# Values folded per head in 16 parts instead of 15 chunks, and the first piece of the down weight clipped on VectorE, scaled and placed by ScalarE

## The chip, the cores and the metric

The kernel runs on one core of one Trainium2 chip. The metric is the device time of one execution in microseconds (us), and the median of several executions is compared. The engines are TensorE (PE, with its weight loads shown as PEld), VectorE (DVE), ScalarE (ACT), GpSimd (POOL) and SyncE (SP), which here only issues transfers (DMA).

## The reference, cut to what matters

The block is a gated cross-attention followed by a feed-forward layer with ternary weights, over 4 batches of 2048 tokens of width 512. The context of a batch has 77 keys of width 384, and there are 8 heads of width 64.

```python
x = x + tanh(g_xattn[0]) * xattn(layernorm(x), ctx_768, Wq, Wk, Wv, Wo, bo)
x = x + tanh(g_ffn[0]) * ffn(layernorm(x), w_gate, w_up, w_down)
# xattn: softmax(q k^T / 8) v per head, then @ Wo + bo
# ffn:   h = relu(bitlinear(x, w_gate))**2 * bitlinear(x, w_up); bitlinear(h, w_down)
def act_quant(x):
    scale = 127.0 / clip(max(abs(x), axis=-1), EPS, None)
    return clip(round(x * scale), -128.0, 127.0) / scale
def weight_quant(w):
    scale = 1.0 / clip(mean(abs(w)), EPS, None)
    return clip(round(w * scale), -1.0, 1.0) / scale
```

Each weight matrix of the feed-forward layer has one unit, the mean of its magnitudes, so no element can be rounded before all of the matrix has been read.

## The kernel before, in words

The 8192 tokens are 64 tiles of 128 tokens. Two things are folded ahead of the tiles. For every batch the keys are multiplied into Wq (`fold_keys`, a matrix "a" of 512 by 616, since 8 heads by 77 keys are 616 columns), and the values into Wo (`fold_values`, a matrix of 616 by 512). Attention of a tile is then two products: tokens with "a" (`make_scores`), probabilities with the folded values (`attend`). Both run on fp32 operands split into a high and a low part.

The folded matrices of batch 0 go straight to where they are used (`first_keys`, `first_values`, and the `_low` functions on VectorE). Those of batches 1 to 3 are evacuated from PSUM by ScalarE (`take_keys`, `take_values`) into small slots of SBUF and stored to DRAM by SP (`store_keys`, `store_values`), to be loaded again when their batch begins (`load_keys`, `load_values`). `fold_values(b, c)` works on a chunk of up to 128 of the 616 rows: GpSimd first writes a matrix `v_pairs` with zeros in which each head's values have rows of their own (`place_values`), and a chunk takes one or two matmuls of 128 rows, depending on how many head pairs it touches. There are three slots for evacuated chunks, in the later-used tile `x1`.

The three feed-forward weights come in 4 pieces of 1 MB each, and every piece passes through four stages: it is loaded, its magnitudes are summed (`measure`, on ScalarE or VectorE), once the unit is known it is scaled with a rounding constant added (`scale`, on ScalarE or VectorE), and two VectorE instructions remove the constant, clip to plus and minus one and write bf16 (`ternary`). The unit of matrix m (0 gate, 1 up, 2 down) comes from `sum_rows(m)`, a matmul `total(m)` and `find_unit(m)`. A piece of the down weight is loaded into the place that a piece of the up weight has left, which ties `load_down` to `ternary(1, ...)`. `relu_half` of the first tile writes its result into the same memory as piece 0 of the down weight, and so waits for `ternary(2, 0)`.

Nothing is scheduled by a planner. Each engine has a list written out by hand for the time ahead of the tiles, and then steps, one per tile, numbered from `s.opens(0)` for tile 0. In step t PE does the first half of gate and up for tile t (`gate_up(s, 0)`), attention of tile t+1, scores of tile t+3, the second half of gate and up, and the down product of tile t-1. Steps 0 and 1 have lists of their own on VectorE (`first_step`, `second_step`), step 1 also on ScalarE. Semaphores hold the order between engines; on an engine the list order is strict, so an instruction that waits holds back all behind it. SP's list is strict as well, and it contains the transposing transfers (`turn_probs` for the probabilities, `turn_input`, `turn_hidden`). On ScalarE the probabilities pass through `part_probs` (planes), the transposing transfer, `join_probs` (probs_t) and `probs_high` (pt_high).

## Time and profile before

| | us |
|---|---|
| median of 3 runs | 1191.43 (1191.32 to 1191.89) |
| profiled execution, its own time | 1190.42 |
| span of the profiled execution, first to last instruction | 1188.6 |
| PE busy | 1174.0 (99%) |
| DVE busy | 1033.9 (87%) |
| ACT busy | 869.2 (73%) |
| first gate matmul of tile 0, 1, 2, 3 | 85.13, 99.97, 118.10, 136.20 |

The profiled execution is 1.0 us under the median, and its time is 1.8 us more than its span. Times in the trace count from the start of the span. What lies ahead of 85.13 us is the preparation; from there on PE works on tiles.

### The profile page before, as it was taken

To read this page: it belongs to the slowest core of one execution; us is meant where nothing else is said; L and a number is where in the kernel's file an instruction comes from. 1 tells how busy PE (TensorE), PEld (TensorE's weight loads), DVE (VectorE), ACT (ScalarE), POOL (GpSimd) and SP (SyncE) were. 2 spreads that over 40 slices of the span, in tenths; PEclk is the share of its full clock that TensorE was granted. 3 is DMA by queue.
4 is the path that set the end of the run, shared out by engine and by line. 5 is a ranking of instruction groups with operands and counts; after the bars stand their busy time and mean duration, and the time that the engine had idled before them with its cause. 6 is when DMAs were issued, how large, how long until landed. Compare 5 with 4: busy or idle time off the path is not lost.

```text
span 1188.6 us, 18855 instructions
## 1 busy us (share of the span) xinstructions
PE 1174.0 (99%) x5867; PEld 744.8 (63%) x5867; DVE 1033.9 (87%) x2124; ACT 869.2 (73%) x929; POOL 307.2 (26%) x313
## 2 busy tenths in 40 slices
PE   9989999999999999999999999999999999999998
PEld 7656656665665666566566656666665666666554
DVE  4989898888988888888998888889899888988887
ACT  5877777776887677677877767776787777677764
POOL 3222222222442222222442222222244222222200
DMA  9793554444444464444444464443444444444333
GB/s 356 262 297 77 156 147 100 98 111 97 97 112 102 126 158 114 96 108 97 101 100 101 115 179 108 98 110 93 101 113 101 100 97 110 97 101 108 84 65 76
DMA packets 286485, 144.71 MB, mean 122 GB/s; under 512 B 254586, under 2 KB 255226, under 8 KB 283889
## 3 DMA queue, kind: packets, MB, share of 16 engines
q1 hardware_dynamic: 286445, 144.32, 47.7%
q8 instruction: 11, 0.18, 0.1%
q14 instruction: 25, 0.20, 0.1%
q10 hardware_dynamic: 4, 0.00, 0.0%
HBM read 57.86 MB, written 24.35 MB: 69 GB/s over the span
## 4 chain that ended last, share of the span: by engine, by line
PE 86%; DVE 7%; ACT 3%; issue 2%; DMA 1%; POOL 0%; DVEq 0%; ACTq 0%; POOLq 0%
PE gu_ps L1084 34%; PE o_ps L1048 17%; PE y_ps L1098 17%; PE s_ps L66 17%; DVE half_max L1330 1%; DVE staged L1324 1%; DMA staged<-in_wd_t 1%; PE gu_ps L1148 1%; PE gu_ps L1208 1%; DMA a_scr<-a_spare 0%; DVE w_up L1484 0%; DVE staged L1456 0%; ACT staged L778 0%; DVE w_down L1484 0%; ACT x_marked L854 0%
## 5 line engine op out<-in xcount | busy, mean ns | idle before, releaser
L1084 PE MATMUL gu_ps<-w_up,xq_t 128*128 128x512 bf16 x1024 | 241.9, 379 | 1.9 <-DVE staged L1324 1.9
L1084 PE MATMUL gu_ps<-w_gate,xq_t 128*128 128x512 bf16 x1016 | 240.9, 380 | 1.3 <-DMA xq_t<-xq 1.2
L1098 PE MATMUL y_ps<-w_down,hq_t 128*128 128x512 bf16 x1008 | 227.8, 379 | 0.0
L1048 PE MATMUL o_ps<-v_sb,pt_high 128*128 128x512 f32 (+1 forms) x640 | 212.8, 413 | 0.9 <-DVE pt_low L1313 0.9
L1324 DVE TENSOR_TENSOR staged<-staged,gu_ps 128x1024 f32<-128x1024 f32 x128 | 155.6, 1216 | 53.5 <-ACT staged L784 53.5
L66 PE MATMUL s_ps<-a_sb,xf_high 128*128 128x308 f32 x1024 | 187.4, 305 | 0.0
L1084 PEld LDWEIGHTS gu_ps<-w_up,xq_t 128*128 128x128 bf16 x1024 | 100.0, 98 | 123.6 <-DVE staged L1324 3.8
L645 POOL TENSOR_TENSOR rstd<-var_eps,neg_half 128x1 f32<-128x1 f32 x128 | 96.4, 753 | 307.1 <-DVE var_eps L1289 274.6
L824 ACT ACTIVATE staged<-staged,h_scale 128x1024 f32<-128x1024 f32 x126 | 137.9, 1142 | 48.9 <-DVE h_scale L1344 48.9
L1098 PEld LDWEIGHTS y_ps<-w_down,hq_t 128*128 128x128 bf16 x1008 | 98.8, 98 | 118.8
L778 ACT ACTIVATE staged<-gu_ps 128x1024 f32<-128x1024 f32 x127 | 128.9, 1015 | 52.4 <-PE gu_ps L1084 52.0
L1084 PEld LDWEIGHTS gu_ps<-w_gate,xq_t 128*128 128x128 bf16 x1016 | 94.3, 98 | 113.5 <-DMA xq_t<-xq 2.8
L66 PEld LDWEIGHTS s_ps<-a_sb,xf_high 128*128 128x128 f32 x1024 | 159.7, 188 | 6.0 <-issue 0.5
L1330 DVE TENSOR_REDUCE half_max<-staged 128x1 f32<-128x1024 f32 x128 | 155.4, 1214 | 2.3
L791 ACT ACTIVATE planes<-probs 128x1280 int16<-128x1280 int16 x63 | 80.0, 1269 | 104.7 <-POOL probs L650 104.7
L626 POOL TENSOR_TENSOR xf_low<-xf_sb,xf_high 128x512 fp32r<-128x512 f32 x64 | 82.7, 1292 | 275.9 <-ACT xf_high L694 275.9
L650 POOL TENSOR_TENSOR probs<-probs,prob_inv 128x616 f32<-128x616 f32 x64 | 78.3, 1223 | 257.1 <-DVE prob_inv L1308 257.1
L1048 PEld LDWEIGHTS o_ps<-v_sb,pt_high 128*128 128x128 f32 (+1 forms) x640 | 120.6, 189 | 34.5 <-issue 1.4
L784 ACT ACTIVATE staged<-staged 128x1024 f32<-128x1024 f32 x128 | 134.8, 1053 | 2.2
L1048 PE MATMUL o_ps<-v_sb,pt_low 128*128 128x512 f32 (+1 forms) x320 | 127.1, 397 | 0.0
L66 PE MATMUL s_ps<-a_sb,xf_low 128*128 128x308 f32 x512 | 113.9, 303 | 0.0
L800 ACT ACTIVATE probs_t<-planes_t 128x1280 int16<-128x1280 int16 x63 | 104.1, 1652 | 0.4 <-DMA planes_t<-planes 0.4
(146 smaller groups left out, 1438.8 us busy)
## 6 DMA issues: line engine op xcount, KB each, us to landing
xf_sb<-in_x_feat SPq DMA_DIRECT2D x64, 256.0 KB, 2.6
x_sb<-in_x_tok SPq DMA_DIRECT2D x64, 256.0 KB, 2.9
y<-staged SPq DMA_DIRECT2D x63, 256.0 KB, 2.0
staged<-in_wg_t SPq DMA_DIRECT2D x4, 1024.0 KB, 9.5
staged<-in_wd_t SPq DMA_DIRECT2D x4, 1024.0 KB, 7.6
folded<-a_scr SPq DMA_DIRECT2D x3, 1232.0 KB, 5.6
v_scr<-x SPq DMA_DIRECT2D x12, 256.0 KB
folded<-v_scr SPq DMA_DIRECT2D x3, 1024.0 KB, 5.1
```

The costliest lines, as they stand in the source:

```text
L66: last = nc.tensor.matmul(s_ps[:, n, 0:HALF_KEYS], x_part[:, c, :], a_sb[:, a, c, n * HALF_KEYS:(n + 1) * HALF_KEYS], start=(c == 0 and x_ ...
L626: nc.gpsimd.tensor_tensor(xf_low[:, s.par(d), :, :], xf_sb[:, :, :], xf_high[:, s.par(d), :, :].bitcast(F32), ALU.subtract).then_inc(xf_lo ...
L645: nc.gpsimd.tensor_tensor(rstd[:, :], var_eps[:, :], neg_half[:, :], ALU.pow).then_inc(done, 1)
L778: nc.scalar.activation(relu, last_gate_ps if at_end else gate_ps, ACT.Relu).then_inc(relu_done[n], 1)
L784: nc.scalar.activation(relu_sq, relu, ACT.Square).then_inc(square_done[n], 1)
L800: nc.scalar.activation(probs_t_halves, planes_t_by_half, ACT.Copy).then_inc(probs_joined, 1)
L824: nc.scalar.activation(h_marked[:, cols], hidden[:, cols], ACT.Copy, bias=ROUND, scale=h_scale[:, 0:1]).then_inc(h_marked_done[n], 1)
L1048: last = nc.tensor.matmul(o_ps[:, :], pt[0:rows, P * c:P * (c + 1)], v_sb[0:rows, v, c, :], start=(c == 0 and pt is pt_high and v == 0), s ...
L1084: last = nc.tensor.matmul(target[:, q, :], xq_t[:, s.par(0), c, :], w[:, c, cols], start=(c == 0), stop=(c == DC - 1))
L1098: last = nc.tensor.matmul(y_ps[:, :], hq_t[:, c, :], w_down[:, c, :], start=(c == 0), stop=(c == FC - 1))
L1324: nc.vector.tensor_tensor(hidden[:, cols], relu_sq, last_up_ps if at_end else up_ps, ALU.mult).then_inc(hidden_done[n], 1)
L1330: nc.vector.tensor_reduce(half_max[:, n:n + 1], hidden[:, cols], axis=AX, op=ALU.max, apply_absolute_value=True).then_inc(half_max_done, 1)
```

## The change

It has five parts.

The values of batches 1 to 3 are no longer folded through `v_pairs`. A part k (of 16) is half the keys of one head, over the three batches together: 231 keys in 116 and 115 rows. Its matmul contracts the head's 64 rows of `v_t` directly, so there are 16 matmuls with 64 rows of contraction where there were 24 with 128, and GpSimd's `place_values` is done once instead of four times. A part spans two batches, so it is stored with two transfers of 77 and 39, or 38 and 77, rows: 32 stores instead of 15. The evacuated parts have seven places: three in `x1`, and four more in `bo_sb`, `probs_t` and `k_pairs` (in the first use order 0, 1, 2, 3, 4).

The first piece of the down weight is loaded into `v_pairs`, which is free once batch 0 is folded, and no longer waits for an up piece. VectorE clips it to plus and minus the unit in one instruction (`clip_first_down`); ScalarE scales it (`mark_first_down`) and later takes the rounding constant off, writing bf16 (`place_first_down`). `relu_half` of tile 0 now waits for `ternary(1, 2)`, the up piece that last used its memory, and the first `down` waits for PLACED.

SP queues all eight gate and up pieces at once, ahead of the first wait. Which engine measures or scales which piece changes: VectorE measures 6 and scales 5 (before 4 and 7), ScalarE measures 6 and scales 6 plus the two new passes (before 8 and 5). The lists ahead of the tiles are reordered on all engines.

ScalarE gets its own `first_step`, and VectorE's `first_step` is reordered. `second_step` and all later steps are as before. In DRAM the folded values now lie row by row.

```diff
-V_OUT_RING = 3
+V_PLACE = [0, 1, 2, 3, 4, 0, 1, 2, 3, 4, 0, 1, 2, 3, 5, 6]
...
+def head_part(k):
+    h, s = divmod(k, 2)
+    return h, KEYS + FIRST_ROWS * s, FIRST_ROWS - s
...
         def raw(m, p):
+            if m == 2 and p == 0:
+                return v_pairs[:, :, :].rearrange("p q n -> p (q n)")[:, 0:PIECE]
...
                 def load_down(p):
-                    sp.wait_ge(weight_stage[1][UP_SLOT.index(p)], DONE)
+                    if p == 0:
+                        sp.wait_ge(vo_done, KC)
+                    else:
+                        sp.wait_ge(weight_stage[1][UP_SLOT.index(p)], DONE)
...
+                def store_later_values(k):
+                    at = KEYS * head_part(k)[0]
+                    sp.wait_ge(vo_taken, k + 1)
+                    for b, j, n, r in part_runs(k):
+                        sp.dma_start(v_scr[b, at + j:at + j + n, :].rearrange("p (q n) -> p q n", q=HP),
+                                     v_slots[V_PLACE[k]][r:r + n, :, :]).then_inc(v_stored[V_STORE[k]], 16)
...
+                def fold_later_values(k):
+                    h, first, rows = head_part(k)
+                    if k < V_RING:
+                        pe.wait_ge(v_split_done, KC + k - V_RING + 1)
+                    else:
+                        pe.wait_ge(vo_taken, k - V_RING + 1)
+                    own = slice(HEAD * (h % 2), HEAD * (h % 2 + 1))
+                    nc.tensor.matmul(value_slots[(KC + k) % V_RING][0:rows, :], v_t[own, h // 2, first:first + rows], wo_sb[own, h // 2, :],
+                                     start=True, stop=True, tile_position=(HEAD * (h % 2), 0)).then_inc(vo_done, 1)
...
+                def clip_first_down():
+                    nc.vector.tensor_scalar(neg_unit[:, :], unit[:, 2:3], -1.0, None, ALU.mult).then_inc(unit_done, 1)
+                    dve.wait_ge(unit_done, 4)
+                    dve.wait_ge(weight_stage[2][0], MEASURED)
+                    nc.vector.tensor_scalar(raw(2, 0), raw(2, 0), unit[:, 2:3], neg_unit[:, 0:1],
+                                            ALU.min, ALU.max).then_inc(weight_stage[2][0], 1)
...
                     if s.opens(0) and n == 0:
-                        wait(act, weight_stage[2][0], DONE)
+                        wait(act, weight_stage[1][UP_SLOT.index(0)], DONE)
...
+                def first_step(s):
+                    relu_half(s, 0)
+                    square_half(s, 0)
+                    mark_first_down()
+                    scale(2, 2)
+                    part_probs(s, 2)
+                    scale(2, 3)
+                    mark_input(s, 1)
+                    join_probs(s, 2)
+                    probs_high(s, 2)
+                    high_part(s, 4)
+                    relu_half(s, 1)
+                    square_half(s, 1)
+                    place_first_down()
+                    exponentials(s, 3)
```

On ScalarE, this is the end of the preparation and step 0 of the kernel before (L812 `probs_high`, L791 `part_probs`, L778 and L784 `relu_half` and `square_half`, L730 `scale`, L800 `join_probs`, L854 `mark_input`, L694 `high_part`).

```order
L812 ACTIVATE pt_high<-probs_t 128x640
L791 ACTIVATE planes<-probs 128x1280
L778 ACTIVATE staged<-gu_ps 128x1024
L784 ACTIVATE staged<-staged 128x1024
L730 ACTIVATE staged<-staged,inv_unit 128x2048 x2
L800 ACTIVATE probs_t<-planes_t 128x2x640
L812 ACTIVATE pt_high<-probs_t 128x640
L854 ACTIVATE x_marked<-centred,x_scale 128x512
L694 ACTIVATE xf_high<-xf_sb 128x512
L778 ACTIVATE staged<-gu_ps 128x1024
L784 ACTIVATE staged<-staged 128x1024
```

The same place of the changed kernel (L858 `probs_high`, L813 `exponentials`, L823 and L829 `relu_half` and `square_half`, L764 `mark_first_down`, L757 `scale`, L836 `part_probs`, L900 `mark_input`, L846 `join_probs`, L721 `high_part`):

```order
L813 ACTIVATE probs<-probs,rstd 128x616
L823 ACTIVATE staged<-gu_ps 128x1024
L829 ACTIVATE staged<-staged 128x1024
L764 ACTIVATE v_pairs<-v_pairs,inv_unit 128x2048
L757 ACTIVATE staged<-staged,inv_unit 128x2048
L836 ACTIVATE planes<-probs 128x1280
L757 ACTIVATE staged<-staged,inv_unit 128x2048
L900 ACTIVATE x_marked<-centred,x_scale 128x512
L846 ACTIVATE probs_t<-planes_t 128x2x640
L858 ACTIVATE pt_high<-probs_t 128x640
L721 ACTIVATE xf_high<-xf_sb 128x512
L823 ACTIVATE staged<-gu_ps 128x1024
```

The planes of tile 2 were made ahead of the first relu; now they come after it, its square and two passes over a weight piece.

On VectorE, this is step 0 of the kernel before from the second half of its list on (L1423 `unmark_input`, L1302 `shift_scores`, L1330 `top_half`, L1484 and L1487 `ternary`, L1324 `hidden_half`, L1313 `probs_low`, L1337 to L1344 `hidden_scales`).

```order
L1423 TENSOR_SCALAR xq<-x_marked 128x512
L1302 TENSOR_TENSOR probs<-s_ps,score_max 128x616
L1330 TENSOR_REDUCE half_max<-staged 128x1
L1484 TENSOR_SCALAR w_down<-staged 128x2048
L1487 TENSOR_SCALAR w_down<-w_down 128x2048
L1324 TENSOR_TENSOR staged<-staged,gu_ps 128x1024
L1313 TENSOR_TENSOR pt_low<-probs_t,pt_high 128x640
L1484 TENSOR_SCALAR w_down<-staged 128x2048
L1487 TENSOR_SCALAR w_down<-w_down 128x2048
L1330 TENSOR_REDUCE half_max<-staged 128x1
L1337 TENSOR_REDUCE h_max<-half_max 128x1
```

The same place of the changed kernel (L1369 `top_scores`, L1399 `hidden_half`, L1377 `shift_scores`, L1388 `probs_low`, L1405 `top_half`, L1567 and L1570 `ternary`, L1412 `hidden_scales`):

```order
L1369 TENSOR_REDUCE score_max<-s_ps 128x8
L1399 TENSOR_TENSOR staged<-staged,gu_ps 128x1024
L1377 TENSOR_TENSOR probs<-s_ps,score_max 128x616
L1388 TENSOR_TENSOR pt_low<-probs_t,pt_high 128x640
L1405 TENSOR_REDUCE half_max<-staged 128x1
L1567 TENSOR_SCALAR w_down<-staged 128x2048
L1570 TENSOR_SCALAR w_down<-w_down 128x2048
L1567 TENSOR_SCALAR w_down<-staged 128x2048
L1570 TENSOR_SCALAR w_down<-w_down 128x2048
L1405 TENSOR_REDUCE half_max<-staged 128x1
L1412 TENSOR_REDUCE h_max<-half_max 128x1
```

Three pieces of work (the shift of the scores, the first half's maximum and one ternary piece) stood ahead of the second `hidden_half`; now all of them stand behind it.

## Rows read from the trace of the kernel before

**Rows 1.** The page's first line and its busy times by engine.
```profile
span 1188.6 us, 18855 instructions
PE 1174.0 (99%) x5867; PEld 744.8 (63%) x5867; DVE 1033.9 (87%) x2124; ACT 869.2 (73%) x929; POOL 307.2 (26%) x313
```

**Rows 2.** Windows: stretch, its length, busy time by engine, granted clock, DMA share, GB/s.
```profile
0.00:85.13 85.13, 78.35 (x354) 56.19 (x354) 62.60 (x97) 58.37 (x81) 27.04 (x41) 1.00 0.88 306
...
154.59:1188.00 1033.41, 1028.92 (x5182) 646.94 (x5180) 907.56 (x1902) 758.41 (x795) 264.64 (x257) 1.00 0.44 107
```

**Rows 3.** Timeline of PE: start, busy, instruction, in brackets idle before and releaser.
```profile
85.13 1.90 PE L1084 MATMUL gu_ps<-w_gate,xq_t 128*128 128x512 bf16 x8
...
118.10 1.90 PE L1084 MATMUL gu_ps<-w_gate,xq_t 128*128 128x512 bf16 x8
```

**Rows 4.** Timeline of ACT around step 0.
```profile
76.76 1.91 ACT L720 ACTIVATE hq_t<-staged 128x2048 bf16<-128x2048 f32 x1 [3.19 <-DMA staged<-in_wd_t]
...
88.07 1.03 ACT L778 ACTIVATE staged<-gu_ps 128x1024 f32<-128x1024 f32 x1 [0.34 <-DVE w_down L1487]
...
90.10 3.89 ACT L730 ACTIVATE staged<-staged,inv_unit 128x2048 f32<-128x2048 f32 x2
93.89 1.65 ACT L800 ACTIVATE probs_t<-planes_t 128x1280 int16<-128x1280 int16 x1
95.58 0.74 ACT L812 ACTIVATE pt_high<-probs_t 128x640 fp32r<-128x640 f32 x1
...
96.89 0.61 ACT L694 ACTIVATE xf_high<-xf_sb 128x512 fp32r<-128x512 f32 x1
```

**Rows 5.** Timeline of DVE, preparation.
```profile
23.73 1.51 DVE L1491 TENSOR_TENSOR a_sb<-gu_ps,a_sb 128x616 fp32r<-128x616 f32 x2 [2.06 <-ACT a_sb L736]
...
49.56 0.15 DVE L1467 TENSOR_SCALAR unit<-y_ps 128x1 f32<-128x1 f32 x1
...
69.29 2.23 DVE L1446 TENSOR_REDUCE part_sums<-staged 128x4 f32<-128x2048 f32 x1
71.44 0.68 DVE L1357 TENSOR_TENSOR x<-x_sb,o_ps 128x512 f32<-128x512 f32 x1
...
74.87 0.79 DVE L1294 TENSOR_REDUCE score_max<-s_ps 128x8 f32<-128x616 f32 x1
...
76.41 0.20 DVE L1384 TENSOR_SCALAR x_top_n<-x_top,rstd 128x1 f32<-128x1 f32 x1
```

**Rows 6.** Timeline of DVE, step 0.
```profile
97.36 0.79 DVE L1302 TENSOR_TENSOR probs<-s_ps,score_max 128x616 f32<-128x616 f32 x1
98.07 1.21 DVE L1330 TENSOR_REDUCE half_max<-staged 128x1 f32<-128x1024 f32 x1
99.20 1.22 DVE L1484 TENSOR_SCALAR w_down<-staged 128x2048 bf16<-128x2048 f32 x1
...
101.06 1.21 DVE L1324 TENSOR_TENSOR staged<-staged,gu_ps 128x1024 f32<-128x1024 f32 x1
102.19 0.82 DVE L1313 TENSOR_TENSOR pt_low<-probs_t,pt_high 128x640 fp32r<-128x640 f32 x1
...
106.03 0.15 DVE L1337 TENSOR_REDUCE h_max<-half_max 128x1 f32<-128x2 f32 x1
...
106.67 0.21 DVE L1344 TENSOR_SCALAR h_scale<-h_inv,hidden_scale 128x1 f32<-128x1 f32 x1
```

**Rows 7.** Groups of instructions by form, 40 to 90 us: busy, mean ns.
```profile
L1208 PE MATMUL gu_ps<-folded,v_pairs 128*128 128x512 f32 x42 | 19.5, 601 | 3.1 <-ACT x L762 3.1
...
L762 ACT ACTIVATE x<-gu_ps,gate_tanh 128x512 f32<-128x512 f32 x12 | 8.0, 677 | 0.3 <-PE gu_ps L1208 0.2
...
L791 ACT ACTIVATE planes<-probs 128x1280 int16<-128x1280 int16 x2 | 2.5, 1266 | 0.0
...
L650 POOL TENSOR_TENSOR probs<-probs,prob_inv 128x616 f32<-128x616 f32 x2 | 2.4, 1217 | 9.0 <-DVE prob_inv L1308 9.0
```

**Rows 8.** The tile planes_t, 0 to 200 us: its transposing transfers.
```profile
DMA to landing us min/median/max: 3.4/3.4/6.5
```

More of the change, by code:

```diff
@@ L912, in step @@
                         mark_hidden(s, -1)
-                    if s.has(0):
+                    if s.has(0) and not s.opens(0):
                         relu_half(s, 0)
@@ L955, in _ @@
                 gate_bias()
-                high_part(start, 1)
                 first_keys(2)
@@ L1645, in _ @@
-                dve.wait_ge(tanh_done, 1)
-                first_values_low(0)
-                measure(0, 3)
-                first_values_low(1)
-                sum_probs(start, 0)
-                sum_rows(0)
-                first_values_low(2)
+                measure(1, 0)
+                sum_rows(1)
+                ternary(0, 0, w_gate)
+                scale(0, 1)
+                find_unit(1)
+                find_hidden_unit()
+                probs_low(start, 0)
+                ternary(0, 1, w_gate)
@@ L1652, in _ @@
+                ternary(0, 2, w_gate)
+                scale(1, 2)
+                scale(1, 0)
+                ternary(1, 3, w_up)
+                ternary(1, 0, w_up)
+                ternary(1, 1, w_up)
+                add_attention(start, 0)
+                input_scale(start, 0)
+                top_scores(start, 1)
+                shift_scores(start, 1)
+                unmark_input(start, 0)
+                sum_probs(start, 1)
+                ternary(1, 2, w_up)
                 dve.wait_ge(rstd1_done, 2)
```

429 lines of the change are left out of this document (219 added, 210 removed).

## The prediction

> **What bounds the kernel now.** I read the page first: PE is busy 1174.0 of 1188.6 us [rows 1]. The windows say where the rest is. From 154.59 us on PE is busy 1028.92 of 1033.41 us, so whatever a change wins or loses before that is passed on almost whole to the end; in the preparation it is busy 78.35 of 85.13 [rows 2]. Everything the change touches in time lies before about 118 us, since the second step and all later ones have the lists they had. So I follow three marks: R, the start of the first relu (88.07 us, [rows 4]); H, the end of the first h_scale, 106.67 + 0.21 = 106.88 us [rows 6]; and the first gate matmul of tile 2, 118.10 us [rows 3]. VectorE passes H on through the unchanged second step (unmark, second `hidden_half`, attention and input scale of tile 2, its transposing transfer), and the gate of tile 2 follows H by 118.10 - 106.88 = 11.2 us.
>
> What stands before R: the last down piece is measured only when it has landed, after ScalarE idled 3.19 us [rows 4]; then come the down unit, two scales and `ternary(2, 0)` on VectorE, and relu waited 0.34 us for that ternary [rows 4]. The preparation is thus bounded by VectorE and the chain of down pieces, not by PE.
>
> **The change part by part.**
>
> Fewer folds. A fold matmul leaves two records: 42 of them took 19.5 us, so one matmul takes 19.5 / 21 = 0.9 us [rows 7]. 24 matmuls become 16. If 64 rows of contraction cost as much as 128, PE saves 8 x 0.9 = 7.2 us; if half, 14. PE idled 3.1 us in front of these matmuls for ScalarE [rows 7], and ScalarE now evacuates 16 parts instead of 15 chunks, 0.7 us more [rows 7]. Since PE does not bound R, I count neither saving. The Trainium skill, TensorEngine Tiling (Array Packing), section Key Properties, says that a change of tiling mode drains TensorE, which speaks against 16 matmuls of 64 rows among matmuls of 128. No row here shows such a drain. It would come out of the 7.2 us that I do not count.
>
> When the up unit is found (t1, 49.56 us, [rows 5]). Ahead of it VectorE now has one more measure (2.2 us, [rows 5]), one `input_stats` less (about 1.1: a pass of 0.7 as in the row at 71.44 and two small ones) and no `probs_low` (0.8, [rows 6]): 0.3 us more work. Against it stand VectorE's waits, such as the 2.06 us at 23.73 [rows 5]. With eight pieces queued without a wait, none of the waits for a landing should last. I take t1 = 48.8, bounds 45 (most of some 4 us of waits gone) and 50.
>
> From t1 to R. VectorE then has, up to the end of the sums of tile 1: small unit instructions 0.8, `probs_low` 0.8, five ternary pieces of 101.06 - 99.20 = 1.9, which is 9.3 [rows 6], two scales of the length of the row at 99.20, 2.4 [rows 6], attention and input scale 74.87 - 71.44 = 3.4, top and shift 76.41 - 74.87 = 1.5 [rows 5], `unmark_input` with its wait for ScalarE 0.8, the sums 1.0: 20.0 us. Then the chain goes over to ScalarE's strict list: normalise on GpSimd 1.2, planes 1.3 [rows 7], `measure(2, 1)` 2.1, `high_part` 0.6 [rows 4], the last five evacuations (two of keys, three of values) at 0.7 = 3.5 [rows 7], a microsecond of waiting for PE's last folds, probs_t 1.7 and pt_high 0.7 [rows 4], exponential 0.8: 12.9 us. So R = 48.8 + 20.0 + 12.9 = 81.7 at the earliest with t1 as taken. VectorE must in the same time have done the fourth up ternary, statistics, two measures and the shift of tile 2 behind the sums: 1.9 + 1.1 + 4.4 + 1.6 = 9.0 us, under the 12.9 minus the final exponential, so it fits. None of these sums holds a stall, and before the same kind of chain had several between 49.56 and 88.07. I add 2.8 us (two waits of a microsecond or so, and rows that run long beside other engines) and take R = 84.5, which is 3.6 us earlier than before. Bounds: 79 with t1 = 45 and half the stalls, 88 if a landing stays on the path as now.
>
> What leaves the path: `ternary(2, 0)` and the down scales no longer stand before R. Were the new down path slow, it would show only at the first down product, where before the hidden transposes came last; the clip costs one pass of the length 1.2 [rows 6], or 2.2 if it runs at the rate of a measure [rows 5], on VectorE between R's shift and step 0, where its cover is ScalarE's 3.2 us of probs_t, pt_high and exponential. `place_first_down`, 1.9 to 2.0 (3.89 / 2, [rows 4]), stands behind the second square, while VectorE does the work below.
>
> From R to H, step 0. Before: 106.88 - 88.07 = 18.8 us. Now ScalarE does relu and square (90.10 - 88.07 = 2.0), two passes of 3.89 / 2 each (93.89 - 90.10 = 3.8), and only then the planes, 1.3 [rows 4, 7]: R + 7.1. The transposing transfer takes 3.4 to 6.5 us to landing [rows 8]; I take 3.4, since the stores and the two token loads ahead of it are some 8 us old by then: R + 10.6 with its start. `scale(2, 3)` and `mark_input` (2.7 us) hide under it. probs_t 1.7, pt_high 0.7, `high_part` 0.6 [rows 4]: the second relu starts at R + 13.6 although PE has its input since about R + 10. Square ends at R + 15.7. VectorE has nothing else ahead in its list and waits for that square from about R + 12 on. Behind it: `hidden_half` 1.1 (102.19 - 101.06), shift 0.7, `probs_low` 0.7, maximum 1.1 (99.20 - 98.07), two ternary pieces 3.7, maximum 1.2, `hidden_scales` 0.9 (106.88 - 106.03) [rows 6]: 9.5 us. H = R + 25.2. That is 6.4 us more than before. The cause is visible in the order: before, 3.7 us of shift, maximum and ternary filled the time in which ScalarE was not ready, and the planes had been made before the first relu.
>
> Sum: H = 84.5 + 25.2 = 109.7, against 106.88: 2.8 us later, and the gate of tile 2 with it, at 120.9. The profiled execution of 1190.42 us would become 1193.2; on the median, 1.0 higher, 1194.2. Batch loads of the folded values (now 2 KB rows) lie under ten tiles of work and count nothing; if one came late it would show at the first tile of a batch.
>
> SP issues 32 stores for 15, 17 x about 0.45 us = 8 us more of issue, spread over 45 us; the first transposing transfer behind them (tile 2's) waits for planes anyway, so it costs nothing unless SP falls more than 5 us behind.
>
> **The rivals.**
>
> Balance: R at 81.7, as the bare sum says, or a stall less in step 0; then H is 106.9 and the time is 1191.4. It is the forecast without the 2.8 us of stalls.
>
> Faster: the waits of VectorE before t1 vanish. Working without a break it would reach t1 near 45 and, with the bare sum, R = 78; H = 103.2, 3.7 us early: 1187.7. It decides from R = 79.3 on (2.4 us early at H). For it: all eight pieces are queued early, and DMA moved only 306 GB/s over the preparation at a share of 0.88 [rows 2]. Against: the 2.06 us wait is one for ScalarE's key evacuation and a fold, which the change leaves in place [rows 5].
>
> Much slower: the stores hold the loads back. 38 rows are 19 x 2, and 77 are 7 x 11, so such pieces may not use all sixteen DMA engines. If 38 rows lie on two engines, each gets 39 KB; at 306 / 0.88 / 16 = 22 GB/s per engine [rows 2] that is 1.8 us for each of eight such stores, and every load behind waits for those two. Two such delays on the path, at the third down piece and at R, give 3.6 us more: R = 88.1, 1197.8. It takes over from the forecast at R = 86.7, where H is 5 us late. The Trainium skill, DMA: Bandwidth & Descriptors, section Why a DMA increments its semaphore by 16 and not by 1, says just this of the split: the largest number up to 16 that divides the outer size, which is 2 for 38 rows, 11 for 77 and 13 for 39. The stores before had 128 and 104 rows, and no row of this trace shows a piece on few engines.
>
> The change does not do what it says: should folds of 64 rows take 0.9 us and evacuations stay as many, the fold part changes nothing on the path; this is already in the forecast.
>
> **How the numbers follow.** A measurement of this kernel tells 0.2% (2.4 us) from no change. Forecast 0.60, with its own range 1191.9 to 1196.5 (H + 0.5 to + 5), of which 0.36 lie above 1193.8 and 0.24 below; balance 0.12; faster 0.13; much slower 0.15. So slower 0.36 + 0.15 = 0.51, same 0.24 + 0.12 = 0.36, faster 0.13. The range goes from 1189.0, inside the faster case, to 1198.5, past the much slower one.
>
> **What would show it.** Right: relu of tile 0 near 84.5 us, a wait of ScalarE's probs_t for planes_t and of VectorE's second `hidden_half` for the square (3 to 5 us) in step 0, an h_scale near 109.7, the gate of tile 2 near 120.9, and the same spacing from there on. Wrong: relu before 80 us or after 87; a transposing transfer of 5 us or more in step 0 (1.6 us more); stalls of folds on `v_stored`; late landings of down pieces. If the gate of tile 2 is late but the end is not, PE made it up later, which would overturn the first step of the argument.

## The result, and the profile after

The changed kernel takes 1194.31 us (median of 18 executions, 1192.11 to 1196.87) where the kernel before took 1191.34 (18, 1188.74 to 1192.93): a ratio of 1.0029, 95% interval 1.0022 to 1.0035, or 3.0 us more. The profiled execution of it took 1195.31 us, which is 1.0 above its median, where that of before lay 0.9 below its own; so the two traces are 4.9 us apart, 1.9 more than the medians. Part of that surplus goes with the clock, as the rows below show.

The page of the changed kernel, with the clock that was granted:

```profile
span 1193.5 us, 18761 instructions
...
PE 1169.3 (98%) x5786; PEld 741.2 (62%) x5851; DVE 1036.3 (87%) x2124; ACT 871.7 (73%) x929; POOL 299.5 (25%) x301
...
PEclk9989999999999999999999999999999999999999
```

PE bounds the kernel as in [rows 1]. TensorE's timeline (start, us, instruction, idle time before it and who ended it) has the marks that answer to [rows 3]:

```profile
73.95 1.11 PE L1283 MATMUL gu_ps<-folded,v_t 64*115 64x512 f32 x2
77.06 1.53 PE L1252 MATMUL gu_ps<-k_pairs,folded 128*128 128x154 f32 x8 [2.00 <-ACT folded L793]
78.52 3.76 PE L1283 MATMUL gu_ps<-folded,v_t 64*116 64x512 f32 x4
...
83.04 3.19 PE L1149 MATMUL gu_ps<-w_gate,xq_t 128*128 128x512 bf16 x7 [0.24 <-issue]
86.02 3.00 PE L1149 MATMUL gu_ps<-w_up,xq_t 128*128 128x512 bf16 x8
...
122.98 1.90 PE L1149 MATMUL gu_ps<-w_gate,xq_t 128*128 128x512 bf16 x8 [1.03 <-DMA xq_t<-xq]
```

The gate of tile 2 starts at 122.98 us, 4.9 later than the 118.10 of before, and this is just what the execution is longer by: nothing is made up afterwards. ScalarE, for [rows 4], and then VectorE, for [rows 6]:

```profile
86.27 1.03 ACT L823 ACTIVATE staged<-gu_ps 128x1024 f32<-128x1024 f32 x1 [0.27 <-PE gu_ps L1149]
...
92.08 1.25 ACT L836 ACTIVATE planes<-probs 128x1280 int16<-128x1280 int16 x1
96.10 0.72 ACT L900 ACTIVATE x_marked<-centred,x_scale 128x512 f32<-128x512 f32 x1 [0.86 <-DVE x_scale L1454]
96.91 1.65 ACT L846 ACTIVATE probs_t<-planes_t 128x1280 int16<-128x1280 int16 x1
...
99.75 1.01 ACT L823 ACTIVATE staged<-gu_ps 128x1024 f32<-128x1024 f32 x1
```

```profile
92.54 0.69 DVE L1432 TENSOR_TENSOR x<-x_sb,o_ps 128x512 f32<-128x512 f32 x1 [1.52 <-PE o_ps L1113]
...
101.88 1.22 DVE L1399 TENSOR_TENSOR staged<-staged,gu_ps 128x1024 f32<-128x1024 f32 x1 [2.54 <-ACT staged L829]
...
111.19 0.21 DVE L1419 TENSOR_SCALAR h_scale<-h_inv,hidden_scale 128x1 f32<-128x1 f32 x1
```

R, the first relu, is at 86.27 us (88.07 before). The planes of tile 2 are made at R + 5.8, the second relu at R + 13.5, VectorE waits 2.54 us for the square, and H, the end of h_scale, is at 111.19 + 0.21 = 111.40: H - R is 25.1 us where it was 18.8. One sign that was forecast is missing here: ScalarE's probs_t does not wait for its transposing transfer, since x_marked ahead of it had waited 0.86 us for VectorE. In e1, e3, e4 and e5 the wait is there, about 1.05 us.

One thing stands in this trace that the trace of before has not: the clock fell. Windows of two microseconds (sum, busy time of the engines, then granted clock, DMA share, GB/s):

```profile
74.00:76.00 2.00, 1.06 (x3) 0.22 (x2) 1.97 (x3) 2.00 (x4) 0.55 (x1) 1.00 1.18 135
76.00:78.00 2.00, 0.94 (x7) 0.94 (x8) 2.00 (x2) 1.58 (x3) 1.27 (x1) 1.00 1.38 52
78.00:80.00 2.00, 2.00 (x5) 0.99 (x5) 1.83 (x4) 0.68 (x1) 0.00 (x0) 0.50 0.85 161
...
86.00:88.00 2.00, 2.00 (x6) 0.76 (x5) 2.00 (x3) 1.70 (x2) 0.00 (x0) 0.50 0.38 109
88.00:90.00 2.00, 2.00 (x9) 1.38 (x8) 1.93 (x4) 2.00 (x2) 1.63 (x1) 0.94 0.29 81
```

PE idled 2.00 us ahead of the key fold at 77.06, then the granted clock was 0.50 for ten microseconds, the lower of its two levels (1.2 instead of 2.4 GHz): eight up matmuls took 3.00 us, where all later ones take 1.89. Of the 18 executions 8 had a mean clock of 0.999 and took 1192.11 to 1194.17 us, 1193.4 in the mean; the 10 others had 0.995 to 0.997 and took 1194.22 to 1196.87, 1195.4 in the mean. The profiled one (0.996) is of the second kind; the profile of before shows 1.00 throughout.

### The profile page after: what moved, and what is told of

Its sections match the earlier page's. It is cut to its first block, busy times and chain, and to the rows that moved or that the text cites. A ratio compares the mean times of both kernels' runs of the same rounds, so it can differ in the third digit from the quotient of the medians.

```text
span 1193.5 us, 18761 instructions
## 1 busy us (share of the span) xinstructions
PE 1169.3 (98%) x5786; PEld 741.2 (62%) x5851; DVE 1036.3 (87%) x2124; ACT 871.7 (73%) x929; POOL 299.5 (25%) x301
## 4 chain that ended last, share of the span: by engine, by line
PE 84%; DVE 6%; ACT 3%; DMA 3%; issue 2%; SPq 1%; ACTq 0%; DVEq 0%
PE gu_ps L1149 33%; PE o_ps L1113 17%; PE y_ps L1164 17%; PE s_ps L71 16%; DMA staged<-in_wg_t 2%; DVE half_max L1405 1%; DMA v_scr<-bo_sb 1%; DVE staged L1399 1%; ACT staged L823 1%; DVE w_gate L1567 0%; DVE w_up L1567 0%; ACT probs_t L846 0%; ACT staged L829 0%; DVE pt_low L1388 0%; PE gu_ps L1283 0%
## 5 line engine op out<-in xcount | busy, mean ns | idle before, releaser
L1149 PE MATMUL gu_ps<-w_gate,xq_t 128*128 128x512 bf16 x951 | 227.9, 381 | 7.9 <-DMA xq_t<-xq 1.6
L1399 DVE TENSOR_TENSOR staged<-staged,gu_ps 128x1024 f32<-128x1024 f32 x128 | 155.6, 1215 | 54.4 <-ACT staged L829 54.4
L823 ACT ACTIVATE staged<-gu_ps 128x1024 f32<-128x1024 f32 x127 | 129.0, 1016 | 49.6 <-PE gu_ps L1149 49.6
L836 ACT ACTIVATE planes<-probs 128x1280 int16<-128x1280 int16 x63 | 79.9, 1269 | 107.1 <-POOL probs L680 107.1
L1405 DVE TENSOR_REDUCE half_max<-staged 128x1 f32<-128x1024 f32 x128 | 155.3, 1214 | 2.3
L829 ACT ACTIVATE staged<-staged 128x1024 f32<-128x1024 f32 x128 | 134.8, 1053 | 2.2
L846 ACT ACTIVATE probs_t<-planes_t 128x1280 int16<-128x1280 int16 x63 | 104.0, 1651 | 0.3 <-DMA planes_t<-planes 0.2
```

Of the source, the lines that this page charges most:

```text
L823: nc.scalar.activation(relu, last_gate_ps if at_end else gate_ps, ACT.Relu).then_inc(relu_done[n], 1)
L829: nc.scalar.activation(relu_sq, relu, ACT.Square).then_inc(square_done[n], 1)
L846: nc.scalar.activation(probs_t_halves, planes_t_by_half, ACT.Copy).then_inc(probs_joined, 1)
L1149: last = nc.tensor.matmul(target[:, q, :], xq_t[:, s.par(0), c, :], w[:, c, cols], start=(c == 0), stop=(c == DC - 1))
L1399: nc.vector.tensor_tensor(hidden[:, cols], relu_sq, last_up_ps if at_end else up_ps, ALU.mult).then_inc(hidden_done[n], 1)
L1405: nc.vector.tensor_reduce(half_max[:, n:n + 1], hidden[:, cols], axis=AX, op=ALU.max, apply_absolute_value=True).then_inc(half_max_done, 1)
```

## The experiments

Theory: the change wins time before R and gives back more in step 0, by VectorE's new order and ScalarE's late planes. Rivals: the clock; stores on few DMA engines; TensorE's 64-row mode; ScalarE's new passes. Twelve kernels were run, each timed beside the kernel before. Ratios are to before, with the 95% interval; R, H and the start of tile 2's gate are from one profiled execution each.

| kernel | ratio | interval | R | H | H - R | gate of tile 2 |
|---|---|---|---|---|---|---|
| before | 1 | | 88.07 | 106.88 | 18.8 | 118.10 |
| changed | 1.0029 | 1.0022 to 1.0035 | 86.27 | 111.40 | 25.1 | 122.98 |
| e1 order on VectorE | 1.0005 | 0.9996 to 1.0014 | 83.32 | 105.75 | 22.4 | 117.34 |
| e2 planes first | 1.0061 | 1.0047 to 1.0075 | 91.82 | 114.58 | 22.8 | 126.16 |
| e3 PE busy | 1.0023 | 1.0012 to 1.0034 | 84.12 | 109.21 | 25.1 | 120.79 |
| e4 full rows | 1.0028 | 1.0017 to 1.0039 | 85.05 | 110.14 | 25.1 | 121.71 |
| e5 rows 109, 122 | 1.0020 | 1.0011 to 1.0029 | 84.01 | 109.10 | 25.1 | 120.67 |
| e6 rows 114, 117 | 1.0098 | 1.0083 to 1.0114 | 90.88 | 117.94 | 27.1 | 129.53 |
| e7 e1 and PE busy | 0.9994 | 0.9985 to 1.0003 | 84.71 | 107.14 | 22.4 | 118.73 |
| e8 before, new order | 1.0011 | 1.0002 to 1.0021 | 89.09 | 110.39 | 21.3 | 121.62 |
| e9 e1 and e5 | 1.0008 | 0.9999 to 1.0017 | 84.80 | 107.20 | 22.4 | 118.78 |
| e10 e7 and e5 | 1.0002 | 0.9993 to 1.0011 | 86.82 | 109.25 | 22.4 | 120.83 |
| e11 e9 and planes early | 1.0032 | 1.0019 to 1.0045 | 85.81 | 110.28 | 24.5 | 121.87 |
| e12 first piece on VectorE | 1.0030 | 1.0021 to 1.0040 | 83.29 | 108.84 | 25.6 | 120.07 |

**e1, VectorE's order of step 0.**

```diff
                     top_scores(s, 3)
-                    hidden_half(s, 1)
                     shift_scores(s, 3)
-                    probs_low(s, 2)
                     top_half(s, 0)
                     ternary(2, 2, w_down)
+                    hidden_half(s, 1)
+                    probs_low(s, 2)
                     ternary(2, 3, w_down)
```

> The changed kernel with VectorE's list of the first step in the order of before in one respect: shift, first maximum and the third down ternary stand ahead of the second hidden_half again, and everything else is as changed. Theory A (what VectorE does while ScalarE is not ready is the cost): 3.7 us of work move into the idle time of about 2.5 to 5 us ahead of the second hidden_half, so h_scale comes 3.5 us after R earlier than in the changed kernel, H - R goes from 25.1 to about 21.5, the gate of tile 2 comes near 119.3 us and the time falls from 1194.3 to about 1190.8, a ratio of 0.9995 to before. Theory B (the late planes on ScalarE are the whole cost): the second hidden_half waits for ScalarE as before and what stands behind it is no shorter than what ScalarE and PE need; H - R stays at 24 to 25 and the ratio at 1.002 to 1.003.

The order alone takes the ratio from 1.0029 to 1.0005; theory B's 1.002 is outside the interval, and theory A's 0.9995 just below its lower end. R came at 83.32 in this profile although nothing ahead of it was changed, so H - R is what the edit is judged by. The profiled execution took 1190.33 us, that of before 1190.42. VectorE and GpSimd of this kernel:

```profile
88.37 0.68 DVE L1432 TENSOR_TENSOR x<-x_sb,o_ps 128x512 f32<-128x512 f32 x1
...
97.02 2.27 DVE L1567 TENSOR_SCALAR w_down<-staged 128x2048 bf16<-128x2048 f32 x1
99.32 0.69 DVE L1570 TENSOR_SCALAR w_down<-w_down 128x2048 bf16<-128x2048 bf16 x1
99.93 1.21 DVE L1399 TENSOR_TENSOR staged<-staged,gu_ps 128x1024 f32<-128x1024 f32 x1
...
105.54 0.21 DVE L1419 TENSOR_SCALAR h_scale<-h_inv,hidden_scale 128x1 f32<-128x1 f32 x1
```

```profile
96.94 1.27 POOL L656 TENSOR_TENSOR xf_low<-xf_sb,xf_high 128x512 fp32r<-128x512 f32 x1 [1.88 <-ACT xf_high L721]
98.16 1.89 POOL L675 TENSOR_TENSOR rstd<-var_eps,neg_half 128x1 f32<-128x1 f32 x1
```

The wait for the square is gone and H comes 2.7 us sooner after R, 0.9 short of the 3.6 expected. The rest went into the ternary at 97.02, which took 2.27 instead of 1.22 us while GpSimd worked beside it, and whose neighbour on GpSimd took 1.89 us where the one before it (94.51) took 0.55. The long ternary comes again in e7, e9 and e10, which have this order too (2.26, 2.25 and 2.28); where GpSimd had nothing beside it, the same instruction took 1.22 (at 101.80 here, at 105.59 in the changed kernel). In the kernel before it was GpSimd that came off worse: its power at 98.81 took 1.64 us, and the ternary at 99.20 beside it 1.22. That the two engines hinder each other is read from these coincidences; no run isolates it.

**e2, planes first.**

```diff
+                    part_probs(s, 2)
                     relu_half(s, 0)
                     square_half(s, 0)
-                    mark_first_down()
                     scale(2, 2)
-                    part_probs(s, 2)
                     scale(2, 3)
+                    mark_first_down()
```

> The changed kernel with ScalarE's list of the first step changed back: the planes of tile 2 (part_probs) ahead of the first relu, and mark_first_down behind both scales; VectorE's list as changed. Theory A (planes late cost as much as VectorE's order): H - R falls by 3 us or more and the time by as much, to 1191. Theory B (the sums of tile 2 and GpSimd's normalising are ready only 3 us or so after R in the changed preparation, since VectorE's sum_probs of tile 2 stands behind the clip): the relu is then held up by the planes, R moves from 86.3 to about 90, H - R falls by at most 2, and the time rises by 1 to 3 us, to 1195.5 to 1197 (ratio 1.0035 to 1.005).

Slower, 1.0061, beyond theory B's 1.005, which the interval (from 1.0047) takes in. ScalarE of this kernel:

```profile
90.64 1.27 ACT L836 ACTIVATE planes<-probs 128x1280 int16<-128x1280 int16 x1 [4.51 <-POOL probs L680]
91.82 1.01 ACT L823 ACTIVATE staged<-gu_ps 128x1024 f32<-128x1024 f32 x1
```

ScalarE waits 4.51 us for GpSimd's normalised probabilities with the relu queued behind. H - R falls by 2.4 us, but R comes 5.5 us later than in the changed kernel. In the changed preparation the late place of the planes is what the late sums ask for.

**e3, PE kept busy.**

```diff
+                def keep_busy():
+                    for _ in range(4):
+                        nc.tensor.matmul(y_ps[:, P:3 * P], ones[:, :], wo_sb[:, 0, 0:2 * P], start=True, stop=True)
...
+                keep_busy()
                 fold_keys(3, 3)
```

> The changed kernel with four extra matmuls of 256 float32 columns (product unused, into columns of the bank of y that nobody reads) ahead of the last fold of keys, where PE idled 2.0 us at 75 us. They add work and leave everything else. Theory A (the granted clock fell to 0.50 between 78 and 88 us because PE had idled): the clock stays at 1.00 in every stretch, the two folds and the gate and up matmuls of tile 0 take what they did before (1.9 us for eight records instead of 3.2), R comes 1.5 to 3 us earlier, near 84, the mean granted clock of all executions is 0.999 or more, and the time falls by 1 to 2 us, to 1192.5 to 1193.3 (ratio 1.001 to 1.0018). Theory B (the clock falls by something else, or the drop hides behind ScalarE and VectorE): the same drops are seen, or they go and the time stays within 0.5 us of 1194.3 (ratio 1.0025 to 1.0029).

The ratio, 1.0023, lies between the theories, and its interval takes in both. Between 78 and 88 us the clock stayed at 1.00, and R came at 84.12, 2.2 us earlier, as theory A had it; but the clock fell elsewhere, first behind an idle time of 2.94 us, so the mean clocks are still 0.996 to 0.999:

```profile
98.70 2.69 PE L1149 MATMUL gu_ps<-w_gate,xq_t 128*128 128x512 bf16 x8 [2.94 <-ACT staged L823]
101.18 2.82 PE L1149 MATMUL gu_ps<-w_up,xq_t 128*128 128x512 bf16 x8
...
140.26 3.30 PE L1149 MATMUL gu_ps<-w_gate,xq_t 128*128 128x512 bf16 x8 [2.04 <-DMA xq_t<-xq]
```

**e4, folds over 128 rows.** (Each part then holds the sum of two heads.)

```diff
-                    nc.tensor.matmul(value_slots[(KC + k) % V_RING][0:rows, :], v_t[own, h // 2, first:first + rows], wo_sb[own, h // 2, :],
-                                     start=True, stop=True, tile_position=(HEAD * (h % 2), 0)).then_inc(vo_done, 1)
+                    nc.tensor.matmul(value_slots[(KC + k) % V_RING][0:rows, :], v_t[:, h // 2, first:first + rows], wo_sb[:, h // 2, :],
+                                     start=True, stop=True).then_inc(vo_done, 1)
```

> The changed kernel with its 16 later value folds contracted over all 128 partitions and without a tile position; so each part holds the sum of two heads' values, not the one head's. Columns, rows of the result, order and waits are the same. Theory A (64 rows cost no less than 128, and a change of the tiling mode costs TensorE something at each of the changes): a fold goes from 1.11 us to about 0.95, and the issue waits of 0.77 us of key folds behind it to about 0.24; PE is off the path, so the time changes by less than 1 us (ratio 1.0022 to 1.0030). Theory B (64 rows were cheaper after all, and what I read as 1.11 us is the bare duration): folds take 1.1 us or more as well and nothing changes behind them. If PE's folds do lie on the path to R through ScalarE's waits, the time falls by 1 to 2 us.

1.0028, theory A. The fold matmuls as a group (count of records, then shortest, median and longest duration in ns), and the weight loads of a key fold behind such a fold, with the wait ahead of them; the changed kernel first, then e4:

```profile
L1283 PE MATMUL gu_ps<-folded,v_t x30: 589/682/1199, 40.9 to 81.2; 64*115 64x512 f32 x16, 64*116 64x512 f32 x14
...
65.59 1.08 PEld L1252 LDWEIGHTS gu_ps<-k_pairs,folded 128*128 128x128 f32 x8 [0.77 <-issue]
```

```profile
L1282 PE MATMUL gu_ps<-folded,v_t x30: 591/592/1057, 40.7 to 80.4; 128*115 128x512 f32 x16, 128*116 128x512 f32 x14
...
64.23 0.97 PEld L1252 LDWEIGHTS gu_ps<-k_pairs,folded 128*128 128x128 f32 x7 [0.24 <-issue]
```

A record of 64 rows is no shorter at best (589 against 591 ns) and 90 ns longer at the median, and the key weights behind one wait 0.77 us instead of 0.24. So the new folds save TensorE only their number, and a return to 128 rows costs about half a microsecond (0.77 - 0.24); neither reaches the time. The drain that the Trainium skill, TensorEngine Tiling (Array Packing), section Key Properties, describes agrees with this.

**e5 and e6, the rows of the stores.**

```diff
-FIRST_ROWS = ((BATCH - 1) * KEYS + 1) // 2
+FIRST_ROWS = 109
...
-    return h, KEYS + FIRST_ROWS * s, FIRST_ROWS - s
+    return h, KEYS + FIRST_ROWS * s, ((BATCH - 1) * KEYS - FIRST_ROWS) if s else FIRST_ROWS
```

(114 instead of 109 in e6.)

> The changed kernel with each head's 231 later rows parted into 109 and 122 instead of 116 and 115; so its stores have 77, 32, 45 and 77 rows instead of 77, 39, 38 and 77. Result, number of instructions, order and bytes are the same. Theory A (a store uses as many DMA engines as the largest number up to 16 that divides its rows: 38 rows then sit on two engines, 32 on sixteen, 45 on fifteen, and this held back what lies behind): landings of stores and loads between 36 and 90 us get shorter, ScalarE's waits of 1.0 to 1.5 us for a_scr stores go, R comes 1 to 2 us earlier than the 84.1 to 86.3 us seen in the kernels with the changed preparation, and the time falls by 1 to 2 us, to about 1192.8 (ratio 1.001 to 1.002). Theory B (the split over engines does not reach the path): the ratio stays at 1.0022 to 1.0035.

> The same with 114 and 117 rows: stores of 77, 37, 40 and 77 rows. By theory A the eight stores of 37 rows sit on one DMA engine each, 76 KB, which at about 22 GB/s per engine are 3.4 us each, twice what 38 rows cost on two; 40 rows use ten engines. Then R comes 1 to 3 us later than in the changed kernel (86 to 89 us) and the time is 1195.5 to 1197.5 (ratio 1.0035 to 1.005). By theory B nothing changes against the changed kernel (ratio 1.0022 to 1.0035), and the run before this one is like it too.

With 37 and 40 rows (e6) the time is 11.7 us above before, about twice the upper end of theory A. The mean clocks are lower too, 0.989 to 0.993, so part of it goes with the clock. With 32 and 45 rows (e5) the ratio is 1.0020, the upper end of theory A, but its interval and that of the changed kernel overlap. The landings differ clearly (DMA issues between 36 and 90 us: count, KB each, median us from issue to landing; first the changed kernel, then e5, then e6):

```profile
staged<-in_wd_t SPq DMA_DIRECT2D x3, 1024.0 KB, 9.0
a_scr<-a_spare SPq DMA_DIRECT2D x6, 308.0 KB, 6.2
...
planes_t<-planes SPq DMA_TRANSPOSE x1, 5.6
```

```profile
staged<-in_wd_t SPq DMA_DIRECT2D x3, 1024.0 KB, 6.7
a_scr<-a_spare SPq DMA_DIRECT2D x6, 308.0 KB, 4.1
...
planes_t<-planes SPq DMA_TRANSPOSE x1, 3.7
```

```profile
staged<-in_wd_t SPq DMA_DIRECT2D x3, 1024.0 KB, 10.2
a_scr<-a_spare SPq DMA_DIRECT2D x6, 308.0 KB, 7.4
...
planes_t<-planes SPq DMA_TRANSPOSE x1, 7.3
```

The folded values stored are the same bytes in all three; in the order 32 and 45, 38 and 39, 37 and 40 rows the landings in these rows grow. The kernel before, whose stores had 128 and 104 rows, has 7.6 us for the down pieces and 4.5 for a_spare. In e6 ScalarE idles for its spare slot twice over 2.5 us:

```profile
54.04 0.69 ACT L793 ACTIVATE a_spare<-gu_ps 128x616 f32<-128x616 f32 x1 [2.81 <-DMA a_scr<-a_spare]
...
86.06 0.68 ACT L793 ACTIVATE a_spare<-gu_ps 128x616 f32<-128x616 f32 x1 [4.55 <-DMA a_scr<-a_spare]
```

In the changed kernel the waits for such stores are 1.10, 1.50 and 1.50 us (at 50.44, 53.79 and 79.08); in e5 none is left. This is the ordering that the rule of the Trainium skill on the split over engines, DMA: Bandwidth & Descriptors, section Why a DMA increments its semaphore by 16 and not by 1, gives: 16 and 15 engines, 2 and 13, 1 and 10. The number of engines itself stands in no row.

**e7, e1 with PE's two idle times filled.** To the edits of e1 and e3 comes:

```diff
+                def keep_busy_again(s):
+                    for _ in range(12):
+                        nc.tensor.matmul(y_ps[:, P:], xq_t[:, s.par(0), 0, :], w_gate[:, 0, P:512], start=True, stop=True)
...
+                    if s.opens(0):
+                        keep_busy_again(s)
                     if s.has(0):
                         gate_up(s, 1)
```

> The changed kernel with the order of the first run (shift, maximum and third down ternary ahead of the second hidden_half), with the four extra matmuls before the last fold of keys, and with twelve extra matmuls of 384 columns in the first step, between the scores of tile 3 and the second half of gate and up, where PE idled 2.9 us; their products are not used. Theory A (PE's idle times of 2 us and more are what the granted clock falls after, and such falls cost the mean execution about 1.5 to 2 us, since the executions of the first run at a mean clock of 0.999 took 1190.0 to 1190.8 and those at 0.996 to 0.997 took 1191.8 to 1193.5): all executions show 0.999 or 1.000 and lie at 1189.5 to 1190.8, ratio 0.9985 to 0.9995. Theory B (the falls come from elsewhere, or the extra work costs what it saves): the mean clocks keep scattering from 0.995 to 0.999 and the ratio is 1.000 to 1.0015.

0.9994, the lowest ratio of all and no different from before by a measurement that tells 0.2%; the interval meets that of e1 too. The mean clocks are 0.998 to 1.000 (0.995 to 0.999 in e1), so the clock was low for less of the time; but the profiled execution still shows 0.50 between 70 and 72 us, behind an idle time of 0.82 us at 67.88. Theory A holds in part.

**e8, the new order in the kernel before.**

```diff
                     unmark_input(s, 1)
+                    hidden_half(s, 1)
                     shift_scores(s, 3)
+                    probs_low(s, 2)
                     top_half(s, 0)
                     ternary(2, 2, w_down)
-                    hidden_half(s, 1)
-                    probs_low(s, 2)
```

> The kernel before, with VectorE's first step changed in one respect as the change does it: the second hidden_half ahead of shift, first maximum and third down ternary. Preparation, folds, down pieces and ScalarE's order are those of before. Theory A (this order alone is most of what the change costs in the first step): VectorE then idles some 2 us ahead of the second hidden_half, for ScalarE's second square, which ends near 98 us here; what stands behind it is 3.7 us longer; H comes near 109 instead of 106.88, the gate of tile 2 near 120.3 instead of 118.1, and the time rises by 1.8 to 2.8 us, ratio 1.0015 to 1.0024. Theory B (the order costs only with late planes): H stays within 1 us and the ratio within 0.9995 to 1.0008.

VectorE of this kernel:

```profile
100.86 1.22 DVE L1324 TENSOR_TENSOR staged<-staged,gu_ps 128x1024 f32<-128x1024 f32 x1 [2.40 <-ACT staged L784]
...
110.18 0.21 DVE L1344 TENSOR_SCALAR h_scale<-h_inv,hidden_scale 128x1 f32<-128x1 f32 x1
```

H - R is 21.3 instead of 18.8: 2.5 us, nearly all of it the wait of 2.40. The ratio, 1.0011, is below theory A's 1.0015, with an interval (1.0002 to 1.0021) that takes it in, as it does part of theory B's range; H, 3.5 us later than before, of which 1.0 is R, decides for A. So the order costs the same 2.5 to 2.7 us put into the old kernel or taken out of the new one.

**e9 and e10, the edits together.** e9 is e1 with the rows of e5, e10 is e9 with both `keep_busy` edits of e7.

> The changed kernel with VectorE's order of the first run and the parts of 109 and 122 rows, and no extra matmuls. Theory A (order and store sizes act at different places, R and H - R, and so add): the order alone took 2.2 us off (1.0005), the rows alone some 1 us (1.0020); together 1191.0 or a little less, ratio 0.9990 to 1.0000, with R near 83.5 and H near 105.5. Theory B (the rows only helped by chance of where the clock fell): ratio 1.0002 to 1.0010, as with the order alone.

> The same with the extra matmuls of the seventh run too (four before the last fold of keys, twelve in the first step). If the three act each for itself: order -2.2 us, rows -1, filled idle times -0.7, from 1194.5 to 1190.3 or so, ratio 0.9982 to 0.9992 and the fastest of all. Rival: the extra matmuls delayed ScalarE's last key evacuation by 2.0 us in the profile of the seventh run and so give back what the clock saves; then this run is no faster than the one before it (ratio within 0.0005 of it).

e9 gives 1.0008, no better than e1: theory B, so nothing shows that what e5 seemed to win adds. Windows of e9's profiled execution show that the clock fell in the place where PE had idled, and once more at 98 us:

```profile
66.00:68.00 2.00, 0.60 (x2) 0.00 (x0) 1.86 (x6) 1.23 (x3) 0.14 (x1) 1.00 1.03 434
68.00:70.00 2.00, 1.88 (x2) 0.41 (x2) 1.24 (x3) 1.92 (x4) 0.00 (x0) 0.55 0.96 400
70.00:72.00 2.00, 2.00 (x8) 1.94 (x8) 1.93 (x4) 0.69 (x1) 1.51 (x1) 0.50 0.93 354
```

e10 gives 1.0002, inside the intervals of e7 and e9 both, with R at 86.82, behind ScalarE's key evacuation, which waited 2.28 us for PE and its extra matmuls. Between the theories it decides nothing, except that the sum of all three was too hopeful.

**e11, the planes made possible and made early.** To the edits of e9 (order and rows) comes:

```diff
+                sum_probs(start, 2)
                 clip_first_down()
                 probs_low(start, 1)
                 scale(2, 1)
-                sum_probs(start, 2)
...
                     square_half(s, 0)
+                    part_probs(s, 2)
+                    scale(2, 2)
                     mark_first_down()
-                    scale(2, 2)
-                    part_probs(s, 2)
                     scale(2, 3)
```

> As the first of this set (order and rows), and besides the sums of tile 2 on VectorE ahead of the clip, and on ScalarE the planes of tile 2 right behind the first square, ahead of all three weight passes. Theory A (it was the late planes that made ScalarE's second relu late, and the second run failed only because the sums were late): with the sums 2.5 us earlier the planes start near R + 2 to 3 instead of R + 5.9, the second relu moves from R + 13.5 to about R + 11, and the time falls by another 1 to 2 us below the first of this set. Theory B (the order on VectorE leaves nothing to gain there, and passes that move behind the planes delay both ternary pieces): the second relu comes no earlier than R + 13, H - R grows by 1 to 2 us, and the time rises by as much.

Theory B: the ratio goes from e9's 1.0008 to 1.0032 and H - R from 22.4 to 24.5. The planes go at 88.29 (R + 2.5), and yet the second relu comes at R + 15.1. pt_low stands behind the sums now, so attention on PE waits 2.69 us for it, VectorE reaches x_scale late, and ScalarE waits 2.23 us for that ahead of everything else.

**e12, the first down piece back on VectorE.** `scale(2, 0)` in the place of `clip_first_down()`, `ternary(2, 0, w_down)` ahead of `ternary(2, 1, w_down)`, and:

```diff
                     square_half(s, 0)
-                    mark_first_down()
...
                     square_half(s, 1)
-                    place_first_down()
```

> The changed kernel with the new path of the first down piece undone: VectorE scales it in the place of the clip and makes it ternary (3.1 us in all instead of the 1.35 us of the clip), and ScalarE's two passes for it (2.0 and 1.9 us) are gone; slots, loads and the other orders as changed. Theory A (ScalarE's two passes are on the path of the first step: the planes stand behind one of them): planes, join and second relu come 1 to 2 us earlier, H - R falls from 25.1 to 23.5, the time to about 1192.8 (ratio 1.0010 to 1.0018). Theory B (VectorE needs the 1.8 us that it now has more, so that the move to ScalarE is neutral or a gain): H - R stays within 0.7 us of 25.1 and the ratio is 1.0025 to 1.0040.

1.0030, theory B; H - R is 25.6. The planes do come earlier (R + 4.6), after a wait of 0.60 us for GpSimd's probabilities, but x_marked then waits 2.67 us for VectorE, which reaches it later. Clip and placement by ScalarE are neither the loss nor a gain that these runs can tell.

## Why the prediction was right

It said 1194.2 us, 2.8 more than before, and the median is 1194.31, 3.0 more. Step by step:

**PE bounds, and what is late at tile 2 stays late.** Right: 4.88 us at the gate of tile 2, 4.89 in the execution.

**The up unit, t1.** 48.44 us; 48.8 was taken. VectorE still waited 2.51 us for the landing of an up piece, so queueing all pieces early did not end its waits, and the faster rival failed here:

```profile
27.15 2.29 DVE L1521 TENSOR_REDUCE part_sums<-w_up 128x4 f32<-128x2048 f32 x1 [2.51 <-DMA w_up<-in_wu_t]
```

**From t1 to R.** 37.8 us against 35.7. VectorE's part was mis-sized: 22.1 us for 20.0, since two passes that [rows 6] has at 1.22 took 1.82 and 2.32 (GpSimd worked beside both) and a wait of 0.76 for ScalarE's exponential was missing, of which 0.4 had been allowed beside `unmark_input`. In e5, where the clock was below 1.00 only between 68 and 74 us, R is at 84.01, 35.4 after its up unit: the 2.8 us for stalls covered this. The profiled execution is 2.3 us later; in it the clock was at 0.50 from 78 to 88 us, and ScalarE waited 1.50 us for a store at 79.08. In e3, with the same stores and a clock of 1.00 up to R, R is at 84.12 and that wait is gone too, so the two go together. R near 84.5 is what the executions with no fall before R (e3) or a short one (e1 83.32, e4 85.05, e5, e12 83.29) show. Which part of the change brings R forward from 88.07 is not shown: e4, e5 and e12 each put one part back or alter it, and R stays early; the new lists of the preparation were not taken apart.

**From R to H.** 25.2 was worked out, 25.1 measured, and 25.1 again in e3, e4 and e5 (the items behind the square add up to 9.4 as rounded there, to 9.5 from the rows). The planes were placed at R + 7.1 at the end, and ended at R + 7.1; the second relu at R + 13.6, and came at R + 13.5. The forecast was read as R and what follows it. Seen from VectorE the 6.3 us have two parts, and these rows of before and of e5 show them:

```profile
90.49 0.69 DVE L1287 BATCH_NORM_STATS2 stats<-x_sb 128x6 f32<-128x512 f32 x1
```

```profile
89.05 0.67 DVE L1432 TENSOR_TENSOR x<-x_sb,o_ps 128x512 f32<-128x512 f32 x1
...
99.58 1.22 DVE L1399 TENSOR_TENSOR staged<-staged,gu_ps 128x1024 f32<-128x1024 f32 x1 [3.75 <-ACT staged L829]
```

The first part is the wait for the square, 3.75 us in e3 to e5 (2.54 in the profiled execution of the changed kernel, where VectorE itself was late by 1.52). The order alone makes a wait of 2.40 in e8, where the square ends at R + 11.7 and VectorE has nothing else to do from R + 9.4 on. In e5 the late planes put the end of the square at R + 15.5, 3.8 later, and VectorE comes to it at R + 11.8, 2.4 later. With the planes as early as in e8 there would, by this estimate, be no wait there, and with VectorE's old order there is none either (e1). So the two causes do not add, and no share of the 3.75 us can be given to one of them. The second part, 2.6 us, is no cost of step 0 at all. Before, VectorE came to step 0 at 90.49 us, 2.4 after R, and needed 16.4 to H without a pause. In e5 it comes there at 89.05, 5.0 after R: R moved 4 us and VectorE's work only 1.4, since the old relu had waited for VectorE's ternary and the new one does not. e1, in which VectorE has no pause from 88.37 us on, still has H 22.4 after R. So H is 3.75 - 1.4 = 2.3 us later, and that is the loss; my 3.6 us of gain at R and 6.4 of loss behind it were the same balance with 2.6 on both sides. In absolute times the second square of e5 ends at 99.55 us and that of before at 99.83: the late planes use up what R had gained. The second hidden_half then starts at 99.58 instead of 101.06, 1.5 us earlier, and with 3.7 us of work moved behind it H comes 2.2 later. e2 and e11 show that earlier planes win nothing on these lists.

**What was costed at nothing.** The folds: 64 rows cost no less, as allowed, and e4 shows the mode drain off the path. The clip took 1.35 us (1.2 was taken), hidden as said (e12). The stores were costed at nothing unless SP fell 5 us behind, and the runs correct this step in its reason, not in its size. Stores of 38 and 39 rows did lengthen landings (a_spare 6.2 us, 4.1 in e5), and a store stood on the chain to R (the critical chain of the changed kernel has this piece; e1 and e3 have one of 9.3 and 9.4 us on a_scr, e5 and e9 none):

```profile
65.25 9.53 DMA v_scr<-bo_sb
```

But with other row counts (e5) the time fell by about 1 us, which the intervals do not tell from nothing, and in e9 by nothing. So the mechanism of the much slower rival is real in the landings, with a price near a microsecond or less at 38 rows, where its estimate was 3.6 at R; e6, with R at 90.88, shows that at 37 rows it would have decided.

**What was not in the prediction.** The clock. Executions with a mean clock of 0.999 are 2.0 us above before, the others 4.0; so of the 3.0 us at the median about one goes with the clock, by my estimate. The mechanism that I worked out accounts for 2.3 us (H in e3 and e5), where my sum had 2.8, and the agreement of the median to 0.1 us is partly luck.

## What to carry to other kernels

When a change moves work from one engine to another ahead of a join, follow the engine that ends last there with its own start and its own pauses; a mark on another engine (here the first relu) can come four microseconds earlier while that engine comes only 1.4 earlier. An instruction that waits for another engine belongs behind whatever is ready (shift, maximum, ternary), in a strictly ordered list above all. Look at the landings when a store gets a new row count, and try another split: 37 and 40 rows instead of 38 and 39 cost 8 us here, part of it with a lower clock, at equal bytes.

## What was unexpected of the hardware

TensorE's granted clock fell to 0.50 (1.2 GHz) for 3 to 10 us after some of PE's idle times, not after all: after 2.0 us ahead of 77.06 in the changed kernel, after 2.94 in e3 and e4, after 0.82 in e7, and behind a stretch in which PE was busy 0.60 of 2.00 us in e9; but not after the same 2.94 us in e1 and e5, and not in before, where PE was busy 0.61 of 2.00 us from 78 to 80. What decides stays open. Over the executions of e1 a mean clock lower by 0.002 to 0.003 goes with some 2 us. Unused matmuls in the idle time removed the fall at that place in e3, and the execution had others at 98 and 140 us.

At equal bytes, the row count of stores of 64 to 90 KB alone moves the landing of the 308 KB stores among them in the same queue: the median for a_spare is 4.1 us with 32 and 45 rows (e5), 6.2 with 38 and 39, 7.4 with 37 and 40 (e6), and the longest landing of a store to a_scr 8.0, 9.6 and 11.6.
